# A decoder stack on one core: two preparation steps of causal attention stand elsewhere in TensorE's order

## The reference

```
def _L1_attn_ref(x, W_attn, b_attn, W_proj, b_proj):
    qkv = jnp.einsum('btc,cd->btd', x, W_attn) + b_attn
    q, k, v = jnp.split(qkv, 3, axis=2)
    ...                                        # heads of 8, rotary turn of q and k
    att = jnp.einsum('bhqd,bhkd->bhqk', q, k) * scale
    att = jnp.where(causal[None, None], att, -jnp.inf)
    att = jax.nn.softmax(att, axis=-1)
    y = jnp.einsum('bhqk,bhkd->bhqd', att, v)
    return jnp.einsum('btc,cd->btd', y, W_proj) + b_proj
x = x + _L1_attn_ref(_layernorm(x, axis=-1), ...)
```

## Time and profile before

| | |
|---|---|
| median of 3 runs | 1297.88 us (1297.42 to 1305.83) |
| profiled execution | 1309.87 us, its span 1307.8 us |
| PE busy | 1078.9 us, 83% of the span |
| DVE / POOL / ACT busy | 949.4 (73%) / 797.5 (61%) / 674.1 us (52%) |
| granted PE clock, mean | 0.908 of full speed |

### The profile page before, as it was taken

One profiled execution on the slowest core, in us unless ns is written; L12 is line 12 of the kernel. 1 busy time (PEld: TensorE's weight loads), 2 busy tenths in 40 slices (PEclk: granted clock), 3 DMA queues, 4 the chain that ended last, 5 costly groups with the idle time before them and its releaser, 6 DMA issues. The chain is left out here.

```text
span 1307.8 us, 31831 instructions
## 1 busy us (share of the span) xinstructions
PE 1078.9 (83%) x11265; PEld 822.8 (63%) x11265; DVE 949.4 (73%) x2308; ACT 674.1 (52%) x1306; POOL 797.5 (61%) x895
## 2 busy tenths in 40 slices
PE   1899998788888887699996999994799987299992
PEld 0566665456655555566654767672698887299992
DVE  3488888468999997566643788884699877566664
ACT  2255554334454443345543566655889755166661
POOL 4678887335566662344435777872878687675562
PEclk9999999659999999689995899997799899599996
DMA  9930000000000000000000000000001001467775
GB/s 343 382 132 2 2 2 2 15 7 16 16 16 16 25 10 2 1 1 1 1 1 1 2 3 3 3 3 14 19 8 30 7 27 36 124 198 231 216 212 199
DMA packets 51707, 75.95 MB, mean 58 GB/s; under 512 B 13134, under 2 KB 31699, under 8 KB 51296
## 3 DMA queue, kind: packets, MB, share of 16 engines
q1 hardware_dynamic: 43488, 61.22, 15.0%
q0 software_dynamic: 4544, 8.47, 1.9%
q10 hardware_dynamic: 3520, 4.23, 0.9%
HBM read 41.02 MB, written 31.70 MB: 56 GB/s over the span
## 5 line engine op out<-in xcount | busy, mean ns | idle before, releaser
L637 DVE TENSOR_REDUCE maxes<-bank 128x8 f32<-128x1024 f32 x192 | 233.4, 1215 | 39.1 <-PE bank L429 38.4
L564 ACT ACTIVATE self_probs<-bank 128x1024 f32<-128x1024 f32 x128 | 129.1, 1022 | 47.0 <-PE bank L461 46.5
L795 POOL TENSOR_TENSOR self_k_hi_m<-self_kq_hi,const 128x512 fp32r<-128x512 f32 x64 | 66.6, 1041 | 79.3 <-ACT self_kq_hi L592 79.3
L571 ACT ACTIVATE self_neg_max<-bank 128x512 fp32r<-128x512 f32 x64 | 38.2, 597 | 142.0 <-PE bank L474 142.0
L1547 POOL DMA_INDIRECT returned<-relu_y,relu_slots x78 | 80.9, 1037 | 49.8 <-DVE relu_y L1519 35.4
L1465 ACT ACTIVATE relu_hidden<-bank,cols 128x256 f32<-128x256 f32 x156 | 74.1, 475 | 43.7 <-PE bank L1434 40.5
L1442 PE MATMUL bank<-relu_w_tiles,relu_hidden 128*128 128x128 f32 x624 | 94.9, 275 | 0.0
L1442 PEld LDWEIGHTS bank<-relu_w_tiles,relu_hidden 128*128 128x128 f32 x624 | 83.2, 192 | 0.0
L643 DVE TENSOR_SCALAR bank<-bank 128x1024 f32<-128x1024 f32 x64 | 78.2, 1223 | 3.4 <-PE bank L449 3.4
L2429 POOL DMA_INDIRECT routed<-latent_rows,latent_place_i x64 | 63.3, 989 | 24.3 <-issue 22.8
L461 PE MATMUL bank<-self_neg_max,const_r 32*128 32x512 f32 x256 | 64.7, 497 | 8.8 <-DVE bank L643 5.3
(11 more groups left out here) (411 smaller groups left out, 3558.9 us busy)
## 6 DMA issues: line engine op xcount, KB each, us to landing
relu_w_tiles<-in_w_ffn SPq DMA_DIRECT2D x39, 512.0 KB, 3.8
routed<-blank SPq DMA_DIRECT2D x1, 19760.0 KB, 60.5
relu_slots<-routed SPq DMA_DIRECT2D x39, 130.0 KB, 4.2
x_all<-in_x SPq DMA_DIRECT2D x8, 256.0 KB, 8.5
x_before<-x_all SPq DMA_DIRECT2D x8, 256.0 KB
relu_w_tiles<-returned SPq DMA_DIRECT2D x4, 512.0 KB, 8.0
latent_mask_rows<-returned ACTq DMA_DIRECT2D x4, 512.0 KB, 8.5
self_ctx_in<-in_ctx SPq DMA_DIRECT2D x8, 192.0 KB, 2.5
```

What stands on the lines that cost most here:

```text
L564: act.activation(probs[n % 2][:, 2 * pair:2 * pair + 2, :, :].rearrange("p u j q -> p (u j q)"), T[:, 2 * pair * GT:(2 * pair + 2) * GT], ...
L637: dve.tensor_reduce(out.rearrange("p j u -> p u j"), S.rearrange("p (u j k) -> p u j k", u=2, j=U), AX.X, ALU.max, negate=True).then_inc(m ...
L795: pool.tensor_tensor(out[n % 2][:, :, :], src[(n // GB) % 2][:, batch_cols(n)].bitcast(F32).unsqueeze(1).broadcast_to([P, U, P]), slots.un ...
```

## The change

In PE's row of the causal order two steps stand elsewhere: the group step `k^5` (key projection) moves from behind `s0` to behind `T`, and the group step `x^6` (transposed input) from between `s1` and `f1` to behind `w`. The rows of ACT, DVE, POOL and SP stay as they are, and no instruction is added or taken away.

```
     "causal": {
-        "PE": "s0 k^5 T m y f0 s1 x^6 f1 w q^5 v^4",
+        "PE": "s0 T k^5 m y f0 s1 f1 w x^6 q^5 v^4",
         "ACT": "m kh^5 e0 xh^6 e1 k^6 q^5 ln^7 qh^4",
```

## The result

| | before | changed |
|---|---|---|
| median of 19 runs | 1303.48 us (1296.14 to 1313.63) | 1311.32 us (1303.27 to 1317.85) |
| ratio, 95% interval | | 1.0061 (1.004 to 1.0081) |
| profiled execution, its span | 1309.87, 1307.8 us | 1307.73, 1305.6 us |
| distance of the x transposes of consecutive groups, from group 2 on | 22.58 us | 24.06 us |

The change makes the kernel slower by 0.61%, 8.0 us on 1303.48 (5.2 to 10.6; the medians themselves differ by 7.8); the forecast was +8.3 us. The measured time, 1311.32 us, is nevertheless 0.3 us above the range: the kernel before, on which the range stood, has a median of 1303.48 over nineteen runs and not the 1297.88 of the first three.

What follows compares the result with a forecast made beforehand. The prediction took TensorE to bound the causal stage, so added waits lengthen the kernel: six places at 1.39 us (0.05 T, 0.90 k, 0.44 y) give +8.3 us on the 1297.88 us median, 1306.2 us, range 1299 to 1311.

Steps and rivals of the forecast that it cites:

- What bounds the stage: Causal stage: PE, busy 19.62 of 20 us, so an added PE wait lengthens the kernel; one place stands for six.
- Part 1: x behind f1 and w: e1 stands behind xh on ACT, so T waits for e1 and PE is held 1.60 us.
- Part 2: k behind T: m comes 0.95 us later, and y waits 0.44 for ACT's copy of k from their shared PSUM bank.
- the bounds: Untraced costs per place, such as k to m at 0.90 or about 0.1 less; sum between 5.1 and 9.6 us.
- The sum: Six places, each 0.05 for T, 0.90 for k and 0.44 for y, 1.39 us together: +8.3 us.
- so the median should become 1306.2 us: Whole kernel: the +8.3 us added to 1297.88 us, the median of the runs before, a rise of 0.6%.
- Rival A: At each place PE saves 0.20 + 0.09 us from fewer tiling changes, nothing holding T: -1.7 us, 1296.1; chance 0.08.
- Rival B: The wait is partly absorbed by slack in a later slot: cost 0 to 5 us, about 1301; chance 0.12.
- Rival C: PE's clock falls to half in the new hole, about 1.6 us at each place: 1311 or more; chance 0.05.

Runs made afterwards that it cites:

- third experiment: The changed kernel with ScalarE's copy xh moved behind e1 in ACT's row; ratio 1.0013 to the kernel before, distance 22.89 us.
- The second: The kernel before with only k moved behind T, x staying between s1 and f1; ratio 1.0037 to the kernel before, distance 23.00 us.
- the fourth: The changed kernel with k one step further back, behind m and directly ahead of y; ratio 1.0103 to the kernel before (four runs), distance 24.45 us.
- the fifth: The kernel before with only k moved, one slot earlier, behind w; ratio 0.9965 to the kernel before, median 1301.58 us, distance 22.53 us.
- run 8: Not a run number: "the third run 8 us" means the third of the first three timed runs of the unedited kernel before, 1305.83 us.

## Why the prediction was right and where it was wrong

**What bounds the stage: right.** An added wait on PE lengthened it in full, and one place stands for all: the distances of the changed kernel are 24.05 or 24.06 from group 2 on.

**Part 1, the wait of T: right**, in place, cause and size (4.01 for 4.00). The third experiment shows the cause: with e1 ahead of xh the wait is gone. It can't be read from the row that was edited; it comes from a row that wasn't, ACT's.

**Part 2, k's new price and y's wait: right** (y 6.94 for 6.92). The second and third experiments have this wait without the other one, the fourth makes it longer, and the fifth, where s0, T and m lie between k and y, has none. Of the bounds, k to m proved to be the lower value: 0.81 (754.11 to 754.92) instead of 0.90. That is no gain, since y waits for the copy: m starts earlier and y does not, so the wait itself is longer than forecast, 0.54 (1.03 from m to y instead of 0.49) for 0.44.

**The sum: right in kind, a term short.** +8.3 for a measured 8.0 (5.2 to 10.6) and 8.9 by the six places of the trace; that 8.3 and 8.0 are so close is partly luck, as the width of the interval says. The missing 0.09 a place is nearly all f0's later start behind a waiting y; I had let f0 follow y as in a slot without a wait.

**The step that failed: "so the median should become 1306.2 us".** The term that was mis-sized is the one the +8.3 was added to. The prediction took 1297.88 us, the median of the three runs shown, as if it were known, and the kernel before measured 1303.48 over nineteen, 5.6 us more; and the range added room for the runs' spread "at the upper side" of only 4.8 us. The prediction itself had the contrary evidence: the profiled execution lay 12.0 us above that median, and the third run 8 us. With the median of the nineteen the same sum gives 1311.8, and measured were 1311.32. The range had to cover both the change and the uncertainty of a median of three runs that spread over 8.4 us, hence some 5 us more at the top. The mechanism stands as it was.

**Rival A** (the strips pay and nothing holds T): its saving exists. From s1's L429 to s0 the stretch with x in it is 2.24 (749.01 to 751.25) instead of 2.44 (756.84 to 759.28), the 0.20 of the forecast; k to m is 0.09 shorter. "TensorEngine Tiling (Array Packing)" of the Trainium skill, section Key Properties, says that a change of tiling mode drains TensorE, and both stretches agree in direction. But PE gets to its wait sooner by just that much. The rival's own condition, that nothing holds T, was not enough either: in the third experiment T isn't held and m comes 0.39 a place sooner, more than the rival's 0.29, but y's wait takes all of it back and the kernel is not faster than before. An order that keeps both savings and has neither wait was not tried. **Rival B** (absorbed later): no; in a distance of 24.06 nothing is given back. **Rival C** (the clock falls in the hole): no; from 730 to 880 us both executions are at 1.00 throughout, hole or not.

## What to carry to other kernels

When a step moves on one engine in a program of fixed orders, look at the unmoved rows of the engines that consume its result: what stands behind the consumer in its queue moves too. A step that shares a buffer with another needs as much unrelated work between them as the copy that frees the buffer takes, here 0.44 + 0.69 + 0.14 us from the start of k's last product (754.68 to 755.95). And where a program has long stretches outside the change, compare a repeating distance inside the changed stage rather than two spans, and give a forecast in absolute time the full uncertainty of the few runs it starts from.

## What the runs showed of the hardware

Two executions of one program differed by 14.8 us in span, with the causal stage's distance the same to 0.01 us. Over the 60 executions of the kernel before that stand beside the experiments the mean granted clock is 0.898 to 0.917 and the time 1295.12 to 1314.2 us; the longer ones tend to have the lower clock (correlation -0.70).

How much hangs on one rise of the clock shows at the start of the causal stage. In the changed kernel and in the fourth experiment PE stands idle for 6.5 us ahead of the first x, and runs at half clock behind it. From 710 to 720 us the changed kernel is granted 0.50, though PE is busy all the time, and the fourth experiment 0.72:

```profile
710.00:720.00 10.00, 10.00 (x88) 7.15 (x90) 3.78 (x7) 5.74 (x7) 5.87 (x8) 0.50 0.00 1
```

```profile
710.00:720.00 10.00, 9.11 (x90) 5.79 (x88) 6.20 (x10) 3.58 (x6) 5.20 (x5) 0.72 0.01 2
```

From x of group 1 to x of group 2 it is 28.07 us (698.54 to 726.61) in the first and 21.82 in the other (709.67 to 731.49). In the first the products take the lengths of full clock from 24.3 us behind x of group 1 on (722.8), in the other from 5.9 us (715.6). So a rise from 1.2 to 2.4 GHz that comes earlier is worth 6.25 us here, most of what the whole change costs: the fourth experiment's whole stage is only 6.1 us longer than before (208.8 us, 696.0 to 904.8), though its six places cost 6 x 1.87 = 11.2. In the first profile of before the rise comes 20.8 us behind x of group 1 (729.8), 3.5 us sooner than in the changed kernel. On the same instructions, from x of group 1 to the last s1 ahead of group 2's place, the changed kernel takes 26.41 us (698.54 to 724.95) and the kernel before 25.28 (708.97 to 734.25): the 1.1 us of the stage that the six places don't explain. Up to their rises the changed kernel and the fourth experiment differ only in that m of batch 0 and k of group 1 are exchanged; whether that brought the rise forward or chance did was not tried. The other two traces with x behind w have 26.91 and 26.93 us, the five with x in its old place 25.65 to 25.77.

And early in these traces the column of the granted clock is not to be trusted: both windows of 58 to 66 us show 1.00, but the same two products stand 0.21 us apart in the one and 0.11 in the other.
